# Attention probabilities normalised on ScalarE instead of GpSimd, with the attention's instruction lists reordered

## The chip, the cores and the metric

The kernel runs on one core of one Trainium2 chip. The metric is device time in microseconds (us) of one execution. Five engines of the core work here, each with its own list of instructions and bound to the others by semaphores: TensorE (PE: matmuls; PEld is its weight load), VectorE (DVE), ScalarE (ACT), GpSimd (POOL) and SyncE (SP), which issues nearly all DMAs.

## The reference, cut to what matters

A gated cross-attention layer and a gated feed-forward layer over x of 8 batches x 128 tokens x 512, in float32. There are 32 query heads of width 128 in 8 groups; each group shares one key and one value head.

```python
q = (layernorm(x) @ Wq)   # 8 x 32 heads x 128 tokens x 128
k = (ctx @ Wk); v = (ctx @ Wv)        # 8 heads each
q = q * cos + rotate_half(q) * sin    # rotary positions, k likewise
scores = einsum('bhqd,bhkd->bhqk', q, k) / sqrt(128)
scores = where(mask == 0, -1e9, scores)
attn = softmax(scores, axis=-1)
x = x + tanh(g_xattn) * (einsum('bhqk,bhkd->bhqd', attn, v).reshape(...) @ Wo)
x12 = layernorm(x) @ w12.T + b12      # then x1, x2 = split(x12)
x = x + tanh(g_ffn) * ((silu(x1) * x2) @ w3.T + b3)
```

## The kernel before, in words

Float32 products are made of three passes of a reduced format (fp32r): each operand is split into a high part `hi` (a copy on ScalarE into the format) and a low part `lo` (source minus hi, on GpSimd or VectorE), and `three` issues hi x hi, lo x hi and hi x lo. So every product costs three matmuls, and every operand one ScalarE copy and one subtraction.

A first stage (to about 118 us) makes the transposed inputs and all of k and v, and parks these in DRAM. Then comes the attention, written out by hand as one list of calls per engine; the position in that list is the only thing that sets the order of the work on an engine. Its piece is a unit: one batch and one group of four heads, 64 units in all, numbered n = 0 to 63; `u(n)` gives the arguments of unit n, and n = 16 gg + 2 c + k. The feed-forward layer follows from about 560 us.

For a unit the engines do, in the order of its data:

- TensorE: `q_block` (12 matmuls; 64 of them, block e needs the rotation of block e - 2 to be done), `scores` (3), `pv` (3), `out_proj` (12).
- VectorE: `cos_q` and `sin_q` (the rotation: one product, and two on 64 partitions), `score_blocks` (for units 4 to 51, whose scores come out transposed: 32x32 blocks are turned into `s_blk`), `mask_turned` (mask and row minimum into `prob`, four instructions) or, for the units outside of these, `mask_scores` (one add and four such instructions), `recip` (the reciprocal of the four row sums), `p_blocks` (32x32 blocks of `prob` turned into `p_blk`), `o_lo_split`, `add_out` (adds to the residual).
- ScalarE: `q_hi_copy`, `exps` (four exps of 128x128 in place in `prob`, with the row sums), `pT_hi_copy`, `o_hi_copy`, `split_chunk` (hi part of a weight chunk).
- GpSimd: `add_q` (sum of the cos and sin products), `q_lo_split`, `norm` (`prob` times the reciprocal of its row sum, one product of 128x512), `pT_lo_split`, and `split_chunk` (lo part of a weight chunk).
- SyncE: `store_s`/`load_s` and `store_p`/`load_p` send the turned blocks through DRAM and back, which finishes the transposition of scores and of probabilities; `next_k`, `next_v` and `load_next_chunk` fetch k, v and weights.

For units 0, 1 and 53 to 63 TensorE transposes `prob` itself (`prob_transpose`), and VectorE makes the lo part of pT. While an engine waits at one call of its list, all calls behind it wait. `prob`, `s_blk`, `p_blk`, q, pT and o have two slots each (k = 0 or 1), so unit n + 2 uses the slot of unit n. `recip` n waits for `exps` n, `norm` n for `recip` n, and `p_blocks` n or `prob_transpose` n for `norm` n.

The calls of the lists that the steps of the prediction touch, at the head of the attention:

```python
# TensorE: scores 0, q 4, q 5, scores 1, T 0, q 6, pv 0, scores 2, q 7, T 1, q 8, scores 3, q 9, pv 1,
#          scores 4, out 0, scores 5, q 10, q 11, pv 2, scores 6, out 1, scores 7, out 2, pv 3
# VectorE: cos_q(6), mask_scores 2, sin_q(6), cos_q(7), sin_q(7), pT_lo 1, recip 2, cos_q(8), sin_q(8),
#          o_lo 0, mask_scores 3, p_blocks 2, score_blocks 4
# GpSimd:  q_lo 2, chunk, add_q 5, norm 1, q_lo 3, chunk, add_q 6, chunk, add_q 7, norm 2, q_lo 4, add_q 8,
#          chunk, q_lo 5, add_q 9, norm 3, chunk, q_lo 6, pT_lo 2, chunk, norm 4, chunk, q_lo 7
```

In the feed-forward part `h_tile(b)` transposes a normalised batch on TensorE, `up(half, m)` is the first layer (24 matmuls), `silu`, `gate`, `gated_hi` and `gated_lo` make the operand of `down` (12 matmuls), and `result` adds the outcome to the residual; `up` i needs `gate` i - 2, and `down` n needs `result` n - 2.

Of the kernel before, what the change touches and what calls it, by code (L numbers as in the profile page):

```python
# [13 lines left out]
GH = H // KVH  # L14
# [64 lines left out]
def build(nc, x, ctx, pos, mask, g_x, g_f, Wq, Wk, Wv, Wo, w12, b12, w3, b3, out):  # L79
# [21 lines left out]
    with es:  # L101
# [105 lines left out]
        act_exp, dve_recip, pool_norm = sems("act_exp", "dve_recip", "pool_norm")  # L207
# [203 lines left out]
        def _(sp):  # L411
# [158 lines left out]
            def ffn_load(t):  # L570

                dst, s, _ = ffn_raw(t)
                if t < RAW:
                    sp.wait_ge(act_whi, CHUNKS - RAW + t + 1)
                    sp.wait_ge(pool_wlo, pool_split(CHUNKS - RAW + t))
                elif t == RAW:

                    sp.wait_ge(act_qhi, 4 * (UNITS - 1))
                    sp.wait_ge(pool_qlo, 4 * (UNITS - 1))
                for i in range(4):  # L580
                    sp.dma_start(dst[32 * i:32 * i + 32, :].rearrange("b (j f) -> b j f", j=4), ffn_src(t, i)).then_inc(s, 16)
            load_next_chunk(0)
            load_chunk(0, 2)
            next_k(0, 1)
            load_next_chunk(1)
            store_p(*u(2))
            store_s(4)
            load_next_chunk(2)
# [3 lines left out]
            store_s(5)  # L592
            load_s(5)
            load_next_chunk(3)
            load_next_chunk(4)
            load_p(*u(3))
            store_p(*u(4))
            store_s(6)
            load_p(*u(4))
            load_next_chunk(5)  # L600
            load_s(6)
            store_p(*u(5))
            store_s(7)
            load_p(*u(5))
            load_s(7)
            store_p(*u(6))
            store_s(8)
            load_p(*u(6))
            load_s(8)
            store_p(*u(7))  # L610
            store_s(9)
            load_p(*u(7))
            next_v(0, 1)
            load_s(9)
            load_next_chunk(6)
            store_p(*u(8))
            store_s(10)
            load_next_chunk(7)
            load_p(*u(8))
            next_k(1, 1)  # L620
            load_s(10)
            next_v(1, 1)
            store_p(*u(9))
            store_s(11)
            load_p(*u(9))
            load_s(11)
            store_p(*u(10))
            store_s(12)
            next_k(0, 2)
            load_s(12)  # L630
            load_p(*u(10))
            load_next_chunk(8)
            store_p(*u(11))
            store_s(13)
            load_next_chunk(9)
            load_p(*u(11))
            load_s(13)
            load_next_chunk(10)
            load_next_chunk(11)
# [4 lines left out]
            load_next_chunk(12)  # L644
# [4 lines left out]
            store_p(*u(14))  # L649
            load_next_chunk(13)  # L650
            store_s(16)
            next_v(0, 2)
            load_p(*u(14))
            load_s(16)
            store_p(*u(15))
            next_k(1, 2)
            store_s(17)
            load_p(*u(15))
            load_next_chunk(14)
            load_s(17)  # L660
            store_p(*u(16))
            load_next_chunk(15)
# [3 lines left out]
            next_v(1, 2)  # L666
            store_p(*u(17))
            store_s(19)
            load_p(*u(17))
            load_s(19)  # L670
            store_p(*u(18))
            store_s(20)
            load_next_chunk(16)
            load_next_chunk(17)
            load_s(20)
            load_p(*u(18))
            store_p(*u(19))
            next_k(0, 3)
            store_s(21)
            load_next_chunk(18)  # L680
            load_p(*u(19))
            load_s(21)
            store_p(*u(20))
            store_s(22)
            load_p(*u(20))
            load_next_chunk(19)
            load_s(22)
            store_p(*u(21))
            store_s(23)
            load_p(*u(21))  # L690
            load_s(23)
            load_next_chunk(20)
            next_v(0, 3)
            store_p(*u(22))
            store_s(24)
            load_next_chunk(21)
            load_p(*u(22))
            load_s(24)
            next_k(1, 3)
            store_p(*u(23))  # L700
            store_s(25)
            load_next_chunk(22)
            load_p(*u(23))
            load_s(25)
            load_next_chunk(23)
            store_p(*u(24))
            store_s(26)
            load_p(*u(24))
            load_s(26)
            store_p(*u(25))  # L710
            next_v(1, 3)
# [3 lines left out]
            store_p(*u(26))  # L715
            store_s(28)
            load_next_chunk(24)
# [5 lines left out]
            load_next_chunk(26)  # L723
            load_p(*u(27))
            load_s(29)
            store_p(*u(28))
            store_s(30)
            load_next_chunk(27)
            next_k(0, 4)
            load_p(*u(28))  # L730
            load_s(30)
            store_p(*u(29))
            store_s(31)
            load_next_chunk(28)
# [4 lines left out]
            store_s(32)  # L739
            load_next_chunk(29)  # L740
            load_p(*u(30))
# [3 lines left out]
            load_next_chunk(30)  # L745
            store_s(33)
            load_p(*u(31))
            load_s(33)
            store_p(*u(32))
            store_s(34)  # L750
            load_next_chunk(31)
            load_p(*u(32))
            load_s(34)
            store_p(*u(33))
            store_s(35)
            next_v(1, 4)
            load_p(*u(33))
            load_s(35)
            store_p(*u(34))
            store_s(36)  # L760
            load_next_chunk(32)
            load_p(*u(34))
            load_s(36)
            load_next_chunk(33)
            next_k(0, 5)
            store_p(*u(35))
            store_s(37)
            load_next_chunk(34)
            load_p(*u(35))
            load_s(37)  # L770
            store_p(*u(36))
            store_s(38)
            load_p(*u(36))
            load_s(38)
            load_next_chunk(35)
            load_next_chunk(36)
            store_p(*u(37))
            store_s(39)
            load_p(*u(37))
            load_s(39)  # L780
            next_v(0, 5)
            store_p(*u(38))
            store_s(40)
            load_p(*u(38))
            load_s(40)
# [2418 lines left out]
```

## Time and profile before

| what | value |
| --- | --- |
| median of 3 runs | 637.25 us (635.72 to 639.18) |
| the profiled execution: its own time | 636.77 us |
| the profiled execution: its span | 634.9 us |
| TensorE busy | 623.6 us, 98% |
| VectorE busy | 482.8 us, 76% |
| GpSimd busy | 450.3 us, 71% |
| ScalarE busy | 319.2 us, 50% |
| DMA | 118.38 MB, mean 186 GB/s |

A row of a group of instructions names the line, the engine, the operation, output<-inputs with their shapes and the count, then the busy time in us and the mean of one in ns, then the idle time of the engine just before them and what ended most of it. A row in order of time names the start in us, the duration in us, the engine, the line and the operation; in square brackets stands the idle time before it and its releaser. The line can be that of a helper: L889 to L891 are the three matmuls of `three`, L1422 is every hi copy, L1964 every lo subtraction on GpSimd, L2370 those on VectorE. Matmuls are pipelined and their ends are modelled, so the next one can start before the last one's end. "issue" as a releaser is time in which the engine waited for nothing that the profile shows; a wait for several semaphores can hide there.

### The profile page before, as it was taken

The page shows a single profiled execution, that of the slowest core. Times are in us where ns is not written, and L with a number is a line of the kernel's source. Part 1 is how long each engine was busy: PE and PEld are TensorE (multiplying, and loading weights), DVE is VectorE, ACT ScalarE, POOL GpSimd, SP SyncE. Part 2 cuts the span into 40 slices and gives each one's busy share as a digit, 9 for nine tenths or more (in the row PEclk, how much of TensorE's full clock was granted, in tenths as well). Part 3 has the DMA queues.
Part 4 walks back from the last instruction along what each step waited for, and adds up shares of the span by engine and source line. Part 5 has one row for each costly group of instructions (what it writes and reads, how often), then busy time and mean ns, then how long its engine had stood idle before and what let it go on. Part 6 is the DMA issues. An engine that isn't in the chain of part 4 may idle for free.

```text
span 634.9 us, 10094 instructions
## 1 busy us (share of the span) xinstructions
PE 623.6 (98%) x2865; PEld 511.7 (81%) x2865; DVE 482.8 (76%) x1235; ACT 319.2 (50%) x893; POOL 450.3 (71%) x374
## 2 busy tenths in 40 slices
PE   8999999998999999999999999999999999999997
PEld 7888888876888877787888788888778788888886
DVE  3987675797878878788878788878885998976342
ACT  5435622554764646455455555554634657545310
POOL 6456866898889898888898898988886677601100
PEclk9999999999999999999999999999999999999999
DMA  9997995156587686776677676876645413000002
GB/s 300 324 324 227 295 321 166 70 188 211 178 266 230 201 249 207 240 244 213 196 244 241 211 245 221 261 234 213 216 139 176 131 50 90 0 2 1 0 34 99
DMA packets 133990, 118.38 MB, mean 186 GB/s; under 512 B 9776, under 2 KB 104496, under 8 KB 133936
## 3 DMA queue, kind: packets, MB, share of 16 engines
q1 hardware_dynamic: 132512, 116.69, 57.7%
q0 software_dynamic: 384, 1.05, 0.5%
q8 instruction: 24, 0.39, 0.2%
q14 instruction: 30, 0.25, 0.1%
q10 hardware_dynamic: 1040, 0.00, 0.1%
HBM read 72.89 MB, written 44.83 MB: 185 GB/s over the span
## 4 chain that ended last, share of the span: by engine, by line
PE 69%; DVE 9%; POOL 8%; DMA 7%; issue 4%; ACT 3%; DVEq 0%; POOLq 0%; ACTq 0%; SPq 0%
PE f_bank L889 9%; PE f_bank L891 9%; PE f_bank L890 9%; PE o_bank L889 7%; PE o_bank L891 7%; PE o_bank L890 7%; DMA p<-p_scratch 3%; DVE t_sin L2417 3%; PE pv_bank L889 3%; PE pv_bank L891 3%; PE pv_bank L890 3%; PE s_banks L889 2%; PE s_banks L891 2%; PE s_banks L890 2%; ACT prob L1492 2%
## 5 line engine op out<-in xcount | busy, mean ns | idle before, releaser
L1492 ACT ACTIVATE prob<-prob,small 128x128 f32<-128x128 f32 x256 | 99.6, 391 | 42.0 <-DVE small L2516 27.9
L889 PE MATMUL f_bank<-xT_hi,wq_hi 128*128 128x512 f32 x256 | 100.4, 392 | 0.7 <-DVE t_sin L2417 0.6
L891 PE MATMUL f_bank<-xT_hi,wq_lo 128*128 128x512 f32 x256 | 99.8, 390 | 0.0
L890 PE MATMUL f_bank<-xT_lo,wq_hi 128*128 128x512 f32 x256 | 99.8, 390 | 0.0
L889 PE MATMUL o_bank<-wo_hi,o_hi 128*128 128x512 f32 x248 | 97.9, 395 | 0.5 <-issue 0.4
L891 PE MATMUL o_bank<-wo_hi,o_lo 128*128 128x512 f32 x248 | 97.0, 391 | 0.0
L890 PE MATMUL o_bank<-wo_lo,o_hi 128*128 128x512 f32 x248 | 96.7, 390 | 0.0
L2004 POOL TENSOR_TENSOR q<-t_cos,t_sin 128x512 f32<-128x512 f32 x64 | 83.2, 1304 | 14.1 <-DVE t_sin L2417 13.7
L2417 DVE TENSOR_TENSOR t_sin<-f_bank,rope 64x512 f32<-64x512 f32 x128 | 88.1, 688 | 2.3
L1964 POOL TENSOR_TENSOR q_lo<-q,q_hi 128x512 fp32r<-128x512 f32 x64 | 82.9, 1297 | 9.5 <-ACT q_hi L1422 9.3
L2019 POOL TENSOR_TENSOR pT_lo<-p,pT_hi 128x512 fp32r<-128x512 f32 x51 | 66.2, 1297 | 22.3 <-ACT pT_hi L1422 22.3
L2013 POOL TENSOR_TENSOR prob<-prob,small 128x512 f32<-128x512 f32 x64 | 66.7, 1042 | 20.7 <-DVE small L2547 19.9
L1422 ACT ACTIVATE pT_hi<-p 128x512 fp32r<-128x512 f32 x51 | 32.2, 631 | 68.5 <-DMA p<-p_scratch 68.3
L1422 ACT ACTIVATE o_hi<-pv_bank 128x512 fp32r<-128x512 f32 x64 | 37.8, 591 | 50.6 <-PE pv_bank L891 50.3
L889 PEld LDWEIGHTS o_bank<-wo_hi,o_hi 128*128 128x128 f32 x248 | 46.6, 188 | 13.0 <-issue 3.9
L889 PEld LDWEIGHTS f_bank<-xT_hi,wq_hi 128*128 128x128 f32 x256 | 48.1, 188 | 10.8 <-issue 0.8
L891 PEld LDWEIGHTS f_bank<-xT_hi,wq_lo 128*128 128x128 f32 x256 | 48.1, 188 | 10.1
L890 PEld LDWEIGHTS f_bank<-xT_lo,wq_hi 128*128 128x128 f32 x256 | 48.1, 188 | 9.8
L891 PEld LDWEIGHTS o_bank<-wo_hi,o_lo 128*128 128x128 f32 x248 | 46.6, 188 | 10.0
L2417 DVE TENSOR_TENSOR t_cos<-f_bank,rope 128x512 f32<-128x512 f32 x64 | 43.7, 684 | 14.0 <-PE f_bank L891 13.7
L890 PEld LDWEIGHTS o_bank<-wo_lo,o_hi 128*128 128x128 f32 x248 | 46.7, 188 | 9.4
L1422 ACT ACTIVATE q_hi<-q 128x512 fp32r<-128x512 f32 x64 | 39.3, 622 | 26.8 <-POOL q L2004 23.5
(185 smaller groups left out, 1439.4 us busy)
## 6 DMA issues: line engine op xcount, KB each, us to landing
p_scratch<-p_blk SPq DMA_DIRECT2D x51, 256.0 KB, 2.1
p<-p_scratch SPq DMA_DIRECT2D x51, 256.0 KB, 3.4
s_scratch<-s_blk SPq DMA_DIRECT2D x48, 256.0 KB, 2.2
s<-s_scratch SPq DMA_DIRECT2D x48, 256.0 KB, 3.4
k_scratch<-ks_parts SPq DMA_DIRECT2D x16, 512.0 KB, 3.1
raw<-in_L_xattn_Wq_dram SPq DMA_DIRECT2D x32, 256.0 KB, 3.9
raw<-in_L_xattn_Wo_dram SPq DMA_DIRECT2D x32, 256.0 KB, 3.5
k_parts<-k_scratch SPq DMA_DIRECT2D x16, 512.0 KB, 4.6
```

The lines of the kernel that those rows point to most:

```text
L889: nc.tensor.matmul(dst, st[0], mv_[0], start=start, stop=False)
L890: nc.tensor.matmul(dst, st[0], mv_[1], start=False, stop=False)
L891: return nc.tensor.matmul(dst, st[1], mv_[0], start=False, stop=stop)
L1422: nc.scalar.activation(dst, src, ACT.Copy).then_inc(s, 1)
L1492: e = nc.scalar.activation(prob[:, k, h, :], prob[:, k, h, :], ACT.Exp, bias=nmin[k][:, h:h + 1], scale=-1.0, accum_out=psum_row[k][:, h:h ...
L1964: nc.gpsimd.tensor_tensor(dst, a, b_, ALU.subtract).then_inc(s, 1)
L2004: nc.gpsimd.tensor_tensor(dst, c, s, ALU.add).then_inc(pool_rope, 1)
L2013: nc.gpsimd.tensor_tensor(prob[:, k], prob[:, k], rrow[k].unsqueeze(2).to_broadcast([128, GH, S]), ALU.mult).then_inc(pool_norm, 1)
L2019: nc.gpsimd.tensor_tensor(heads_by_q_block(pT_lo[:, k]), by_q_block(p32[:, k]), heads_by_q_block(f32(pT_hi[:, k])), ALU.subtract).then_inc ...
L2417: return nc.vector.tensor_tensor(dst, a, b_, ALU.mult)
```

## The change

`norm` moves from GpSimd to ScalarE. Where GpSimd made one product of 128x512 with the reciprocals broadcast, ScalarE makes four copies of 128x128, each with the reciprocal of its head as scale. The semaphore `pool_norm` becomes `act_norm`. All lists of the attention and of the feed-forward part are written anew for it, on all five engines: the same calls with the same arguments, moved by some places. On ScalarE norm n stands behind `exps` n, with none to four copies between.

```diff
@@ prob_transpose and p_blocks
-                pe.wait_ge(pool_norm, n + 1)
+                pe.wait_ge(act_norm, n + 1)
-                dve.wait_ge(pool_norm, n + 1)
+                dve.wait_ge(act_norm, n + 1)
@@ ScalarE
+            def norm(gg, c, k):
+                act.wait_ge(dve_recip, n_of(gg, c, k) + 1)
+                for h in range(GH):
+                    p = nc.scalar.activation(prob[:, k, h, :], prob[:, k, h, :], ACT.Copy, scale=rrow[k][:, h:h + 1])
+                p.then_inc(act_norm, 1)
@@ GpSimd
-            def norm(gg, c, k):
-                pool.wait_ge(dve_recip, n_of(gg, c, k) + 1)
-                nc.gpsimd.tensor_tensor(prob[:, k], prob[:, k], rrow[k].unsqueeze(2).to_broadcast([128, GH, S]), ALU.mult).then_inc(pool_norm, 1)
```

The lists of after, at the head of the attention (T is `prob_transpose`):

```python
# TensorE: scores 0, q 4, q 5, scores 1, T 0, q 6, scores 2, pv 0, q 7, T 1, q 8, scores 3, q 9,
#          scores 4, out 0, scores 5, pv 1, q 10, scores 6, q 11, pv 2, out 1, out 2, scores 7, pv 3
# VectorE: cos_q(6), sin_q(6), mask_scores 2, cos_q(7), sin_q(7), o_lo 0, pT_lo 1, cos_q(8), recip 2,
#          mask_scores 3, p_blocks 2, sin_q(8), score_blocks 4
# GpSimd:  q_lo 2, chunk, q_lo 3, chunk, add_q 5, add_q 6, chunk, add_q 7, q_lo 4, q_lo 5, chunk, chunk,
#          q_lo 6, chunk, add_q 8, pT_lo 2, add_q 9, q_lo 7
# ScalarE: norm 0, q_hi 2, q_hi 3, pT_hi 0, chunk, chunk, exps 1, o_hi 0, chunk, norm 1, pT_hi 1, exps 2,
#          q_hi 4, norm 2, chunk, chunk, q_hi 5, exps 3, norm 3, q_hi 6, mask fill, o_hi 1, chunk, q_hi 7,
#          pT_hi 2, exps 4, chunk, norm 4
```

A stretch of ScalarE's list in the middle, as a diff in order (before, then after):

```diff
-exps 25, chunk, pT_hi 24, o_hi 23, q_hi 28, q_hi 29, exps 26, pT_hi 25, chunk, chunk, o_hi 24, exps 27
+exps 25, chunk, norm 25, o_hi 23, q_hi 28, chunk, pT_hi 24, exps 26, q_hi 29, norm 26, pT_hi 25, chunk, o_hi 24, exps 27
```

In the feed-forward part TensorE's list has `up(0, 2)` ahead of `h_tile(4)` where it stood behind `h_tile(5)`, and VectorE's list has `result(0)` and `result(1)` behind `gated_lo(7)`. In the tail of the attention TensorE's list has `prob_transpose` 53, 54 and 55 ahead of the scores of two units on and of the q blocks that they stood behind.

## Rows read from the trace of the kernel before

**Rows 1.** The page's first part: busy us, share of the span, instructions.
```profile
PE 623.6 (98%) x2865; PEld 511.7 (81%) x2865; DVE 482.8 (76%) x1235; ACT 319.2 (50%) x893; POOL 450.3 (71%) x374
```

**Rows 2.** Busy us by stage: length; PE, PEld, DVE, ACT, POOL; clock; DMA, GB/s.
```profile
137.00:160.00 23.00, 20.74 (x89) 16.14 (x88) 18.40 (x50) 11.62 (x37) 19.08 (x17) 1.00 0.67 214
160.00:480.00 320.00, 317.37 (x1385) 257.45 (x1384) 264.20 (x745) 179.15 (x557) 277.69 (x229) 1.00 0.69 222
```

**Rows 3.** TensorE's table of waits: releaser, us in total, times, longest.
```profile
PE pv_bank L889 <- issue: 1.5, 3, 0.9
PE pv_bank L889 <- DVE o_lo L2370: 1.3, 3, 0.7
...
PE o_bank L889 <- issue: 0.4, 2, 0.2
...
PE s_banks L889 <- issue: 0.3, 1, 0.3
```

**Rows 4.** TensorE in order of time, in the head of the attention.
```profile
131.01 0.47 PE L889 MATMUL f_bank<-xT_hi,wq_hi 128*128 128x512 f32 x1 [0.63 <-DVE t_sin L2417]
...
138.70 0.47 PE L889 MATMUL s_banks<-q_hi,k_parts 128*128 128x512 f32 x1 [0.38 <-DVE small L2537]
...
149.40 0.47 PE L889 MATMUL pv_bank<-pT_hi,v_hi 128*128 128x512 f32 x1 [0.92 <-issue]
149.71 0.40 PE L890 MATMUL pv_bank<-pT_lo,v_hi 128*128 128x512 f32 x1
149.94 0.39 PE L891 MATMUL pv_bank<-pT_hi,v_lo 128*128 128x512 f32 x1
...
154.70 0.47 PE L889 MATMUL s_banks<-q_hi,k_parts 128*128 128x512 f32 x1 [0.97 <-POOL q_lo L1964]
```

**Rows 5.** GpSimd in order of time: pT_lo of unit 2.
```profile
148.01 1.29 POOL L2019 TENSOR_TENSOR pT_lo<-p,pT_hi 128x512 fp32r<-128x512 f32 x1
```

**Rows 6.** In order of time: unit 47's pT_lo on GpSimd, its pv on TensorE.
```profile
458.86 1.29 POOL L2019 TENSOR_TENSOR pT_lo<-p,pT_hi 128x512 fp32r<-128x512 f32 x1
...
460.25 0.47 PE L889 MATMUL pv_bank<-pT_hi,v_hi 128*128 128x512 f32 x1 [0.18 <-issue]
```

**Rows 7.** The page's groups of instructions: the exps, the sines, the norm.
```profile
L1492 ACT ACTIVATE prob<-prob,small 128x128 f32<-128x128 f32 x256 | 99.6, 391 | 42.0 <-DVE small L2516 27.9
...
L2417 DVE TENSOR_TENSOR t_sin<-f_bank,rope 64x512 f32<-64x512 f32 x128 | 88.1, 688 | 2.3
...
L2013 POOL TENSOR_TENSOR prob<-prob,small 128x512 f32<-128x512 f32 x64 | 66.7, 1042 | 20.7 <-DVE small L2547 19.9
```

**Rows 8.** ScalarE in order of time: a chunk's copy and the exps behind it.
```profile
265.09 0.62 ACT L1422 ACTIVATE wo_hi<-raw 128x512 fp32r<-128x512 f32 x1
265.61 0.40 ACT L1492 ACTIVATE prob<-prob,small 128x128 f32<-128x128 f32 x1
265.91 0.19 ACT L1492 ACTIVATION_READ_ACCUMULATOR prob<-prob,small 128x1 f32 x1
266.01 0.39 ACT L1492 ACTIVATE prob<-prob,small 128x128 f32<-128x128 f32 x1
```

**Rows 9.** ScalarE's table of waits.
```profile
ACT pT_hi L1422 <- DMA p<-p_scratch: 68.3, 34, 4.0
ACT o_hi L1422 <- PE pv_bank L891: 50.3, 31, 4.3
```

**Rows 10.** In order of time: ScalarE's pT_hi of unit 23, TensorE's pv behind it.
```profile
291.49 0.63 ACT L1422 ACTIVATE pT_hi<-p 128x512 fp32r<-128x512 f32 x1 [3.96 <-DMA p<-p_scratch]
...
294.52 0.47 PE L889 MATMUL pv_bank<-pT_hi,v_hi 128*128 128x512 f32 x1 [0.73 <-DVE o_lo L2370]
```

**Rows 11.** In order of time: gate(0) on VectorE, silu(1) on ScalarE.
```profile
572.38 0.74 DVE L2601 SCALAR_TENSOR_TENSOR t_sin<-f_bank,b_col,t_cos 128x512 f32<-128x512 f32 x1
...
575.50 0.69 ACT L1584 ACTIVATE t_cos<-s_banks,b_col 128x512 f32<-128x512 f32 x1 [0.78 <-PE s_banks L891]
```

**Rows 12.** ScalarE's groups: the one table load ahead of the attention.
```profile
L1422 ACT ACT_TABLE_LOAD x1 | 1.3, 1283 | 1.2 <-PEq L3192 1.2
```

More of the change, by code:

```diff
@@ L2795, in _ @@
             recip(*u(22))
+            add_out(*u(18))
             add_out(*u(19))
+            score_blocks(*u(24))
             p_blocks(*u(22))
-            score_blocks(*u(24))
             o_lo_split(*u(20))
@@ L2816, in _ @@
             o_lo_split(*u(22))
+            recip(*u(25))
             cos_q(0, 31)
-            recip(*u(25))
             sin_q(31)
             p_blocks(*u(25))
-            add_out(*u(22))
-            score_blocks(*u(27))
-            mask_turned(*u(26))
-            o_lo_split(*u(23))
-            recip(*u(26))
-            cos_q(0, 32)
-            sin_q(32)
+            mask_turned(*u(26))
+            score_blocks(*u(27))
+            o_lo_split(*u(23))
+            cos_q(0, 32)
+            recip(*u(26))
+            sin_q(32)
+            add_out(*u(22))
+            add_out(*u(23))
             p_blocks(*u(26))
-            add_out(*u(23))
             score_blocks(*u(28))
@@ L2833, in _ @@
             cos_q(0, 33)
+            sin_q(33)
             recip(*u(27))
-            sin_q(33)
+            add_out(*u(24))
             p_blocks(*u(27))
-            add_out(*u(24))
             score_blocks(*u(29))
@@ L2842, in _ @@
             recip(*u(28))
-            sin_q(34)
             p_blocks(*u(28))
+            mask_turned(*u(29))
+            score_blocks(*u(30))
             add_out(*u(25))
-            score_blocks(*u(30))
-            mask_turned(*u(29))
             o_lo_split(*u(26))
@@ L2965, in _ @@
             score_blocks(*u(45))
+            mask_turned(*u(44))
             o_lo_split(*u(41))
[L2967 removed]
             cos_q(0, 50)
[L2969 removed]
             recip(*u(44))
@@ L2972, in _ @@
             p_blocks(*u(44))
+            add_out(*u(40))
+            score_blocks(*u(46))
             add_out(*u(41))
-            score_blocks(*u(46))
             o_lo_split(*u(42))
@@ L3011, in _ @@
             o_lo_split(*u(47))
-            sin_q(55)
+            score_blocks(*u(51))
             p_blocks(*u(49))
-            score_blocks(*u(51))
             mask_turned(*u(50))
+            recip(*u(50))
+            add_out(*u(46))
             cos_q(0, 56)
-            recip(*u(50))
-            sin_q(56)
-            add_out(*u(46))
             p_blocks(*u(50))
             add_out(*u(47))
+            sin_q(56)
             mask_turned(*u(51))
```

1155 lines of the change are left out of this document (577 added, 578 removed).

## Prediction

> **What bounds the kernel now.** I read the busy shares of the engines first, then the same by stage, then TensorE's own waits, and last single stretches in order of time. TensorE is busy for 623.6 of 634.9 us [rows 1], at the full granted clock, and the head and the middle of the attention leave it only 2.3 and 2.6 us idle [rows 2]. So the change can't make the kernel faster by taking work off another engine; it can only remove moments in which TensorE stands still, or add some. Its table of waits and its rows in order of time hold them [rows 3, 4]. The reader adds up, in the attention and behind it: three waits of pv that the table puts down to issue, 1.5; three for the o_lo split, 1.3; one of 0.97, 0.63 and 0.38 each in the head; two of out_proj, 0.4; and three small ones of the scores of 0.3, 0.3 and 0.2, of which one row stands. That is 6.0 us in 14 waits. A wait costs more than its idle time. In a running stream a matmul starts 0.23 us after the one before, though it lasts 0.39; behind a wait the first lasts 0.47 and the second starts 0.31 later [rows 4]. Idle time is counted from the modelled end of the last matmul, 0.39 after its start, so each wait loses its idle time and 0.16 + 0.08 = 0.24 us more; 14 x 0.24 = 3.4. All that can be won is about 9.4 us, 1.5% of the time; the profiled execution took 636.77 us, and 627.4 would be its floor.
>
> **Where the waits lie.** Four are in the head, 0.63 + 0.38 + 0.92 + 0.97 = 2.90 us idle, with 0.24 each 3.9 us [rows 4]: q_block 8 at 131.01 waits for sin_q(6); scores 4 at 138.70 for mask_scores 3; pv 2 at 149.40, whose last input, pT_lo 2, starts at 148.01 and ends at 149.30 [rows 5]; scores 7 at 154.70 for q_lo 7. Two small ones follow at 460.25 and 461.49, of 0.18 and 0.31, 1.0 us in all; the first begins 0.1 us after GpSimd ended the pT_lo that it needs [rows 6], the second likewise after a q_lo. The three o_lo waits cost 2.0 in all. GpSimd is the fullest engine after TensorE: 277.69 of 320 us, 87%, in the middle, VectorE has 264.20, 83%, ScalarE 179.15, 56% [rows 2].
>
> **The norm itself.** Removed: 64 GpSimd products of 1042 ns, 66.7 us [rows 7], one for each unit. A unit has 12 + 3 + 3 + 12 = 30 matmuls 0.23 us apart, 6.9 us; GpSimd's load falls by 1.04 / 6.9, from 87% to 72%. Added: 256 ScalarE copies of 128x128, four a unit. The trace has no copy of that form with a scale read from a column. Bounds: four can't be quicker than one 128x512 copy, behind which the next instruction starts 0.52 us later; and they cost at most what four exps do, whose starts are 0.40 us apart with the readout of the sum between them, 1.6 us [rows 8]. The readout starts 0.30 us behind its exp, where a next copy would start; the exp has one column operand, as the new copy has. I take 4 x 0.30 = 1.2 us of ScalarE, nearest to that row, 77 us in all, and 1.3 us to the end of the last one.
>
> The Trainium skill speaks of that price too ("ScalarE: Activation LUTs", What ACT_TABLE_LOAD costs): an ACTIVATE has a fixed part of 186 ns, an operand read from a column adds 93 ns, an element 0.83 ns, and neighbours overlap by 93 ns. That is an estimate of 386 ns for one and 1.27 us for four, where the exp of the trace agrees with 391 ns [rows 7]; it speaks against four short instructions in the place of one. By it alone each unit's path grows by 0.2 us, and as that is covered (below) the sum stays what it is by the rows.
>
> What of it is on the path: unit n's path from scores to pv runs over s_blk, two DMAs, mask_turned, exps, recip, norm, p_blk, two DMAs, pT_hi, pT_lo. On GpSimd the norm had to wait for the operation in hand there, up to 1.3 us when it came at a bad moment. In the new ScalarE list it stands right behind its exps, mostly with nothing or one copy between. So + 0.2 us of work, and less queueing: the path gets no longer. What it adds is a wait inside ScalarE's list: norm n waits for recip n, which waits for exps n. Where VectorE is free that turn takes the 0.18 of the reciprocal and some 0.1 on each side, 0.4 us; where it is inside the two sines, up to 2 x 0.69 more [rows 7]. Queued behind it are q_hi, o_hi, pT_hi and the weight chunks; for these GpSimd and VectorE wait, and then TensorE. A unit now holds 0.56 x 6.9 = 3.9 us of ScalarE; + 1.2 + 0.4 makes 5.5, 80% of it. Now the engine idles 68.3 us for the loads of p and 50.3 for pv [rows 9], so there is room, but less of it.
>
> **The reordering in the head.** (1) sin_q(6) moves ahead of mask_scores 2, which is five VectorE operations: the wait of 0.63 is gone. (2) mask_scores 3 moves ahead of sin_q(8), so comes 1.4 us earlier, while scores 4 moves ahead of pv 1, 3 x 0.23 = 0.7 earlier: the wait of 0.38 is gone with 0.3 to spare. (3) pT_lo 2 loses norms 1, 2 and 3 ahead of it on GpSimd, 3.1 us, and p_blk 2 now precedes sin_q(8). But on ScalarE pT_hi 2 is moved behind norm 3, a mask fill, an o_hi, a chunk and a q_hi. Followed step by step with the durations above, pT_lo 2 ends at about 148 and pv 2 comes due about 147.3, with scores 6 now ahead of it: a wait of 0 to 0.6, with its restart up to 0.8. I take 0.8 and keep 0 for the range. (4) q_lo 7 loses norm 4 ahead of it, and scores 7 moves behind out_proj 2, 12 x 0.23 = 2.8 us: gone. The head gives -3.9 + 0.8 = -3.1.
>
> **The rest of the attention.** The two waits near 460: norms 47 and 48 no longer precede their pT_lo and q_lo, so up to -1.0; I take -0.8. Against that stands ScalarE. The model is the wait at 294.52: pT_hi had waited 3.96 us for its load, a chunk, a q_hi and o_hi were queued behind it, then o_lo, and pv lost 0.73 + 0.24 = 0.97 us [rows 10]. Each norm takes 1.6 us of the room in which such a backlog is caught up. I take one more such wait, rounded up to +1.1; the bounds are -2.0 (the three o_lo waits go) and +9.7 (ten of them, below). The other moves (out_proj, add_out, score_blocks, sines by a place, weight loads by up to two units, in the tail the transposes on TensorE ahead of scores) are covered: each operation keeps its unit, and a weight chunk is asked for some eight units, over 50 us, before it is read. A missed cover would show as a wait for raw, or as TensorE waiting for exps, and cost up to a norm, 1.3 us, once.
>
> **SyncE's queue.** Stores and loads of p and s keep their order, moved by a place at most; the k and v reloads and the chunks move past one or two of them. Each has about a unit, 6.9 us, in hand. Nothing; a late one would stop scores or pv once, for 1 to 3 us.
>
> **The feed-forward part.** up(0, 2) moves ahead of h_tile(4). It needs gate(0), which starts at 572.38, 3 us before up(0, 1) ends (silu(1), at 575.50, follows it) [rows 11]. h_lo(7) is then due with the end of up(0, 3), 24 x 0.23 = 5.5 us behind the last h_tile; three h_lo, gated_lo(0), a tile, gate(2) and a bias of about 0.7 each stand before it and leave some 0.7 us. result(0) goes behind gated_lo(7), some 4 us after the last up ends; down(2) needs it at 5.5. Nothing; without that cover up to 1 us each.
>
> **Sum.** -3.1 - 0.8 + 1.1 = -2.8 us: 636.77 - 2.8 = 633.97 for the profiled execution. The median of the runs, 637.25, lies 0.48 above it, so I predict 637.25 - 2.8 = 634.45, given as 634.4.
>
> **Rivals.** (B) No new waits, and the o_lo waits go as well, since a looser GpSimd lets TensorE's list run as planned: -3.1 - 0.8 - 2.0 = -5.9, 631.3. For it: GpSimd at 87%. Against it: such waits follow late loads, which no order cures. (C) The gain is handed back: four waits of the form of 294.52, 4 x 0.97 = 3.9, 637.2. For it: ScalarE at 80% in a fixed order. (D) Slower: ScalarE becomes the late engine. In its list pT_hi waits for a load 34 times, up to 4.0 us [rows 9], and the room behind such a wait shrinks by 1.6 us. From seven waits of 0.97 on, 6.8 against 3.9, the kernel is slower by 0.5%; ten give 9.7 - 3.9 = +5.8, 643.0. Against it: pT_hi n - 1 now stands mostly behind norm n, later in the unit, when its load has more often landed. (E) The change pays for switches between Exp and Copy, 128 table loads of 1.28 us, 164 us. Exps and copies alternate already and share one load [rows 12], so 1 in 100.
>
> **Chances.** The forecast 0.50 (own range 632.4 to 636.4), B 0.20, C 0.18, D 0.11, E 0.01. What a measurement of this kernel can tell from no change is about 0.5%, 3.2 us, so faster means below 634.06: all of B and 0.22 of the forecast's 0.50, 0.42. Slower are D, E and the upper end of C, 0.13. The rest is no difference, 0.45. The range goes from 630.8 to 638.8: it leaves out D and E (0.12) and the outer ends of B and C (0.06).
>
> **What would show it.** GpSimd's busy time falls by 66.7 us, ScalarE's rises by 77 to 100; the copies last about 0.39 us and start 0.30 apart. In TensorE's waits q_block 8, scores 4 and scores 7 are gone from the head and pv 2 is short or gone; waits for q_lo are gone; those for o_lo are as many or one more. If TensorE's waits sum to over 9 us of idle time, with o_lo and the loads of p in the chain behind them, D is right; if to under 1.5, B. The prediction is wrong from the ground up if the distance of the matmuls, 0.23 us, changes.

## The result, and the profile after

The changed kernel took 643.67 us (median of 7 runs, 639.34 to 645.14), the kernel before 637.98 beside it (7 runs): ratio 1.0091, interval 1.0067 to 1.0114. It is slower by 0.9%, 5.7 us, where 2.8 us less were forecast. Its profiled execution, 639.34 us with a span of 637.4, is the fastest of the seven; its trace shows 2.5 us of the loss, measured by the spans.

TensorE's granted clock tells a part of what the trace leaves out. Its mean over a run was 1.00 in three of the seven runs, the profiled one among them, and 0.996 or 0.997 in the other four, the median run among these; all 69 runs of the kernel before in the later rounds had 0.999 or 1.00. A run at 0.997 holds a short stretch at the lower of the clock's two levels, 1.2 instead of 2.4 GHz, which cost some 1.6 us in the one trace taken apart below (e5).

The page's line of busy times of the kernel after, and the group of the moved norm (the columns as ahead of the prediction):

```profile
PE 623.1 (98%) x2865; PEld 511.5 (80%) x2865; DVE 484.9 (76%) x1235; ACT 394.1 (62%) x1149; POOL 386.4 (61%) x310
...
L1499 ACT ACTIVATE prob<-prob,small 128x128 f32<-128x128 f32 x256 | 81.7, 391 | 13.9 <-DVE small L2549 13.8
```

ScalarE gained 74.9 us of work and GpSimd lost 63.9 [rows 1]; a copy lasts 391 ns, and the four of one unit stand in time as

```profile
344.75 1.28 ACT L1499 ACTIVATE prob<-prob,small 128x128 f32<-128x128 f32 x4 [0.25 <-DVE small L2549]
```

so the work moved at the forecast price (1.2 us a unit and 1.3 to its end), and the wait for the reciprocal is 13.8 us in 30 waits for all 64 units, half of the 0.4 us a unit that I had allowed. The loss lies elsewhere. The same two stages as [rows 2], of after:

```profile
137.00:160.00 23.00, 22.78 (x99) 17.89 (x98) 19.26 (x52) 16.85 (x52) 18.81 (x15) 1.00 0.75 239
160.00:480.00 320.00, 312.17 (x1360) 252.45 (x1359) 258.74 (x724) 229.37 (x731) 225.90 (x179) 1.00 0.70 221
```

In the head TensorE idles 0.2 us where it idled 2.3: the forecast gain is there. In the middle it idles 7.8 us where it idled 2.6. TensorE's table of waits of after (releaser, us in total, times, longest), against [rows 3]:

```profile
PE o_bank L889 <- issue: 3.2, 6, 1.4
PE pv_bank L889 <- DVE o_lo L2372: 2.6, 2, 2.3
PE o_bank L889 <- ACT o_hi L1422: 1.7, 1, 1.7
...
PE pv_bank L889 <- issue: 0.5, 2, 0.2
```

The waits are few and some are long, before out_proj and pv. The chain of waits of after, ahead of the two longest (start, us, what); first to out_proj at 235.91, which waited 1.7 us, then to pv at 350.44, which waited 2.3:

```profile
223.93 6.52 DMA p_scratch<-p_blk
...
230.46 2.97 DMA p<-p_scratch
...
233.99 0.61 ACT q_hi L1422
234.60 0.49 ACT o_hi L1422
...
235.91 0.47 PE o_bank L889
```
```profile
339.42 4.94 DMA s_scratch<-s_blk
...
344.38 3.17 DMA s<-s_scratch
...
348.50 0.62 DVE p_blk L2560
349.12 0.60 DVE s_blk L2503
349.72 0.59 DVE o_lo L2372
...
350.44 0.47 PE pv_bank L889
```

Both begin at a store of p or s that landed late, 6.52 and 4.94 us after its issue, against a median of 2.1 and 2.2 in the kernel before. An engine's fixed list does the rest: ScalarE stood at pT_hi for the reload of p, with q_hi and the o_hi of another unit queued behind it; VectorE stood at the mask for the reload of s, with p_blk, s_blk and o_lo behind it. SyncE's own list in order of time says what was on the way when the first of these stores was issued:

```profile
221.74 0.57 SPq L498 DMA_DIRECT2D raw<-in_L_xattn_Wo_dram  x1
222.96 0.37 SPq L543 DMA_DIRECT2D s<-s_scratch  x1
223.38 0.50 SPq L456 DMA_DIRECT2D k_parts<-k_scratch  x1
223.93 0.43 SPq L512 DMA_DIRECT2D p_scratch<-p_blk  x1
```

A weight chunk (256 KB), a reload of s (256 KB) and the keys (512 KB) were issued within 2.2 us ahead of the store. The page's DMA rows say that stores land later in general. Kernel before, then after (count, KB each, median us from issue to landing):

```profile
p_scratch<-p_blk SPq DMA_DIRECT2D x51, 256.0 KB, 2.1
p<-p_scratch SPq DMA_DIRECT2D x51, 256.0 KB, 3.4
s_scratch<-s_blk SPq DMA_DIRECT2D x48, 256.0 KB, 2.2
s<-s_scratch SPq DMA_DIRECT2D x48, 256.0 KB, 3.4
```
```profile
p_scratch<-p_blk SPq DMA_DIRECT2D x51, 256.0 KB, 2.6
p<-p_scratch SPq DMA_DIRECT2D x51, 256.0 KB, 3.1
s_scratch<-s_blk SPq DMA_DIRECT2D x48, 256.0 KB, 2.8
s<-s_scratch SPq DMA_DIRECT2D x48, 256.0 KB, 3.2
```

In the lists themselves, between the stores of units 8 and 46, 57 or 58 loads of weights, keys and values have these neighbours in SyncE's list:

| kernel | behind a unit's reloads, ahead of the next stores | between the two stores | behind the stores, ahead of the reloads | between the two reloads |
|---|---|---|---|---|
| before | 20 | 8 | 22 | 7 |
| after | 34 | 7 | 8 | 9 |

So the first theory is: the new list puts the bulk loads ahead of the stores, the stores land late, and now and then TensorE waits. The rivals: ScalarE is too full (D of the prediction); or the new lists of the engines don't fit each other whatever the transfers do.

### The profile page after: what moved, and what is told of

It reads as the page before. It is cut to its first block, busy times and chain, and to the rows that moved or that the text cites. A ratio compares the mean times of both kernels' runs of the same rounds, so it can differ in the third digit from the quotient of the medians.

```text
span 637.4 us, 10287 instructions
## 1 busy us (share of the span) xinstructions
PE 623.1 (98%) x2865; PEld 511.5 (80%) x2865; DVE 484.9 (76%) x1235; ACT 394.1 (62%) x1149; POOL 386.4 (61%) x310
## 4 chain that ended last, share of the span: by engine, by line
PE 83%; DVE 7%; DMA 6%; issue 2%; ACT 1%; POOL 1%; SPq 0%; DVEq 0%; ACTq 0%
PE f_bank L889 11%; PE f_bank L891 11%; PE f_bank L890 11%; PE o_bank L889 9%; PE o_bank L891 8%; PE o_bank L890 8%; PE pv_bank L889 3%; PE pv_bank L891 3%; PE pv_bank L890 3%; PE s_banks L889 3%; PE s_banks L891 3%; PE s_banks L890 3%; DMA s_scratch<-s_blk 2%; DVE t_sin L2419 1%; PE t_bank L889 1%
## 5 line engine op out<-in xcount | busy, mean ns | idle before, releaser
L1492 ACT ACTIVATE prob<-prob,small 128x128 f32<-128x128 f32 x256 | 99.6, 391 | 47.9 <-DVE small L2518 40.0
L1499 ACT ACTIVATE prob<-prob,small 128x128 f32<-128x128 f32 x256 | 81.7, 391 | 13.9 <-DVE small L2549 13.8
L2372 DVE TENSOR_TENSOR o_lo<-pv_bank,o_hi 128x512 fp32r<-128x512 f32 x64 | 43.5, 680 | 7.0 <-ACT o_hi L1422 6.6
```

What stands on the lines that cost most here:

```text
L1492: e = nc.scalar.activation(prob[:, k, h, :], prob[:, k, h, :], ACT.Exp, bias=nmin[k][:, h:h + 1], scale=-1.0, accum_out=psum_row[k][:, h:h ...
L1499: p = nc.scalar.activation(prob[:, k, h, :], prob[:, k, h, :], ACT.Copy, scale=rrow[k][:, h:h + 1])
L2372: nc.vector.tensor_tensor(dst, src, f32(hi_part), ALU.subtract).then_inc(s, 1)
```

## The experiments

Each ratio is to the kernel before, run beside it on the same chip.

**The lists, one at a time.** e1 and e2 exchange SyncE's whole list between the kernels, the feed-forward loads and the order of stores and reloads included; e3 takes the move back out of the new lists and gives GpSimd its old one, and e4 makes the move alone in the old ones.

```diff
# e1: after, its SyncE list replaced by that of before; e2: before, with that of after
# e3: after, but norm is GpSimd's product again, and GpSimd's list that of before
# e4: before; GpSimd's list without its norms, and on ScalarE:
             exps(*u(n))
+            norm(*u(n))      # one call later for units 2 and 52
```

> The changed kernel, with SyncE's list of before put back; all else as changed. Theory ScalarE (its list is too full, o_hi comes late behind any late load): nothing is mended, 643 to 645. Theory SyncE (in the new list weight, k and v loads are issued in bunches ahead of the stores and loads of p and s, whose round trips then take up to 6.5 us): the late round trips go, and the head's gain of 3 us stays, 633 to 636. Theory TensorE and VectorE lists (less distance between a unit's steps): 643 to 645.

> The kernel before, with only SyncE's list of the changed kernel. Theory SyncE: the late round trips appear here too, 641 to 645. Theory ScalarE, and theory TensorE and VectorE lists: as before, 637 to 639.

> The changed kernel's lists on SyncE, TensorE, VectorE and ScalarE, but the norm is the one GpSimd product again: its calls are taken out of ScalarE's list, and GpSimd has its list of before. Theory ScalarE: the room is back, 634 to 638. Theory SyncE: stays at 641 to 645. Theory TensorE and VectorE lists: stays at 641 to 645.

> The kernel before with all its lists, but norm n on ScalarE as four scaled copies straight behind exps n (one call later for units 2 and 52), and taken out of GpSimd's list. Theory ScalarE: slower than before by 4 to 7 us, 642 to 645, with o_hi and o_lo in the waits. Theory SyncE, and theory TensorE and VectorE lists: not slower, 634 to 638, as GpSimd's waits near 150 and 460 go and SyncE's order is the old one.

| kernel | median us | ratio, interval |
|---|---|---|
| e1_after_old_sync | 653.30 | 1.0275, 1.0239 to 1.0311 |
| e2_before_new_sync | 666.99 | 1.0498, 1.0462 to 1.0535 |
| e3_after_norm_gpsimd | 706.38 | 1.1106, 1.1077 to 1.1135 |
| e4_before_norm_scalar | 657.63 | 1.0330, 1.0301 to 1.0358 |

None of the four came out in a range that any theory had given for it. These exchanges cost 17 to 70 us, many times what is to be explained. They say that the lists belong together; they don't say which one lost the 5.7 us. e4 says one thing more: in the old lists the move costs 21 us, in the new ones 5.7, so the reordering took back most of its price. Where e4 lost it: TensorE's waits of that kernel, and its stages 160 to 480 and 480 to 560 (idle 7.2 and 8.0 us; before 2.6 and 0.5), and ScalarE's wait for the reciprocals, 39.4 us where after has 13.8.

```profile
PE pv_bank L889 <- DVE o_lo L2372: 8.8, 8, 1.8
```
```profile
160.00:480.00 320.00, 312.81 (x1360) 253.25 (x1359) 258.84 (x723) 229.87 (x723) 229.17 (x181) 1.00 0.69 220
480.00:560.00 80.00, 71.97 (x367) 58.62 (x367) 60.02 (x182) 55.72 (x182) 41.06 (x34) 1.00 0.33 95
```
```profile
ACT prob L1499 <- DVE small L2549: 39.4, 63, 4.8
```

**ScalarE's work and its wait, by themselves.** e5 leaves out most of the normalisation (one copy of 128x4 a unit, the wait kept; the probabilities stay unnormalised). e8 adds four copies of 128x128 a unit to the kernel before, from tiles that nobody changes, with no wait. e9 adds the wait and no work.

```diff
# e5, in after                                     # e8, in before, behind exps 4 to 51
-  for h in range(GH): ... prob[:, k, h, :]        +  for h in range(GH):
+  for h in range(1):  ... prob[:, k, h, 0:4]      +      nc.scalar.activation(junk[:, k, h, :], mfill[:, h, :], ACT.Copy, scale=tg_x)
# e9, in before, where e4 has its norms
+  act.wait_ge(dve_recip, n_of(gg, c, k) + 1)
```

> The changed kernel with the norm cut to one copy of 128x4 (only four probabilities of the first head are scaled, the rest stays unnormalised); wait for recip and all lists kept. ScalarE has 0.9 to 1.0 us less of work for each unit. Theory ScalarE work: 633 to 637, the o_hi and o_lo waits mostly gone. Theory DMA (late landings of the p and s stores behind bunched loads): 640 to 643, since the landings don't change.

> The kernel before, norm on GpSimd, with four copies of 128x128 more on ScalarE straight behind the exps of units 4 to 51 (mfill scaled into an unused region; nobody waits for them, they wait for nothing). It is the work of the moved norm without its wait: 48 x 1.2 = 58 us of ScalarE. Theory ScalarE work: slower by 4 us or more, up to the +21 of the norm moved in the old lists. Theory that the wait for recip is what hurts: within 2 us of before.

> The kernel before with its lists and with the normalisation on GpSimd; ScalarE only waits, behind each block of exps, until VectorE has the reciprocals of the row sums (at the places where e4_before_norm_scalar had its four copies). Theory, the wait costs: moving the copies in the old lists cost 21 us although the same amount of ScalarE's work with no wait cost 2.5 us (e8), so this kernel is slower by 10 to 20 us (647 to 657), and the trace shows some 30 to 40 us of waits for the reciprocals on ScalarE. Rival, it is the copies' coming late on ScalarE, or GpSimd's list without them, that cost the 21 us: then this kernel is within 3 us of before (under 640).

| kernel | median us | ratio, interval |
|---|---|---|
| e5_after_short_norm | 640.73 | 1.0078, 1.0048 to 1.0108 |
| e8_before_extra_copies | 639.06 | 1.0036, 1.0011 to 1.0061 |
| e9_before_wait_only | 641.59 | 1.0072, 1.0046 to 1.0098 |

With next to no work of the norm left, the changed kernel is still slower than before by 0.8%; the intervals of e5 and of after overlap. In the kernel before, the same work, for 48 of the 64 units, costs 2.3 us and the wait 4.6 (these two intervals overlap as well). So D, a ScalarE too full, falls as the whole account: the work explains no more than a part of the loss. e8 came out between my two ranges, just above the one for work that hurts nobody (within 2 us). For e9 I had said two things. The time was a miss, 4.6 us and not 10 to 20; the waits were not. The trace books 33.5 us under the reciprocal (L2614), spread over what stands behind it, o_hi 12.2, pT_hi 9.4, the weight chunks' and q's copies the rest. So the 30 to 40 us of waits are there, and most of them cost TensorE nothing. Work and wait by themselves make 7 of e4's 21 us; what makes the rest, of which 7.5 us more idle time stand in the stage 480 to 560, stays open. The clock has a share: e4's six runs have means of 0.992 to 0.999.

e5's trace shows what a long wait costs beyond its idle time, a rival to all accounts by waits alone. TensorE stood for 2.03 us ahead of an out_proj; then the clock fell (the first matmul behind the wait, then a row of busy times by stage as above, with the clock third from its end):

```profile
291.50 0.61 PE L889 MATMUL o_bank<-wo_hi,o_hi 128*128 128x512 f32 x1 [2.03 <-issue]
...
292.00:295.00 3.00, 3.00 (x9) 2.32 (x8) 2.43 (x5) 1.19 (x6) 0.23 (x1) 0.50 0.45 135
```

The matmuls of that stretch start 0.43 us apart, not 0.23. From 291.50 to 295.22 nine of them took 3.72 us, where 2.15 would do at the full clock (0.31 behind the wait, then 8 x 0.23): 1.6 us more for one wait. All four runs of e5 have a mean of 0.997, so part of what it has left is the clock's, and it is no clean price of the norm's work. Not each such wait is followed by it: behind the 2.27 us at 350.44 the trace of after stays at 1.00.

**The traffic.** e6 and e7 load only a quarter of each weight chunk of the attention (the rest of the chunk keeps old values), in after and in before; every issue, wait and place stays.

```diff
-                sp.dma_start(dst, wq_src(G, o) if o < 4 else wo_src(G, o - 4)).then_inc(raw_loaded[o], 16)
+                src = wq_src(G, o) if o < 4 else wo_src(G, o - 4)
+                if o < 4: dst, src = dst[:, 0:1], src[:, 0:1]
+                else:     dst, src = dst[:, 0:128], src[:, 0:128]
+                sp.dma_start(dst, src).then_inc(raw_loaded[o], 16)
```

> The changed kernel with each weight chunk of the attention loaded only to a quarter (the rest of the slot keeps stale weights, so the projections are of other weights); same number of DMAs, same order. Theory DMA: the landings of the p and s stores fall back to 2 to 3 us, longest under 4, and the time to 631 to 635. Theory ScalarE work: 640 to 644.

> The control: the kernel before with the weight chunks loaded to a quarter (stale weights, as in the other). Both theories: 1 to 3 us faster than before, 634 to 637, since its longest waits behind late loads go. If it gains as much as the changed kernel does by the same edit, the loads are no reason for the difference between the two.

| kernel | median us | ratio, interval |
|---|---|---|
| e6_after_small_weights | 632.83 | 0.9945, 0.9926 to 0.9964 |
| e7_before_small_weights | 634.74 | 0.9964, 0.9943 to 0.9986 |

These two part the theories. Less traffic gives the changed kernel 1.5% (1.0091 to 0.9945, 9.3 us) and the kernel before 0.4% (2.3 us), with every instruction of the engines at its place. In e6 the medians to landing are 2.1 and 2.1 us for the stores, 2.9 and 3.0 for the reloads, and the middle idles 2.7 us, as before:

```profile
160.00:480.00 320.00, 317.30 (x1390) 258.61 (x1389) 263.35 (x738) 233.26 (x745) 230.35 (x182) 1.00 0.62 198
```

So the loss hangs on transfers, and with these lighter the new lists are no worse than the old, by the medians 1.9 us better (the two intervals overlap).

**The places of the loads.** The order of the stores and reloads stays in each of these; only where the loads of weights, keys and values stand between them changes. e11 and e12 exchange the places, which changes the order among some loads too; e10, e13, e17 and e18 arrange them anew in after, e14 in before, between units 8 and 48.

```diff
# e10, one load behind the two stores, a second behind both reloads
-            load_next_chunk(16)
             store_p(*u(19))
             store_s(21)
+            load_next_chunk(16)
             load_s(21)
-            load_next_chunk(17)
             load_p(*u(19))
-            next_k(0, 3)
+            load_next_chunk(17)
             store_p(*u(20))
             store_s(22)
-            load_next_chunk(18)
+            next_k(0, 3)
             load_p(*u(20))
# e11: after, each load behind the same store or reload as in before; e12: before, as in after
# e13: as e10, the second between the two reloads;  e14: the rule of e10 in before
# e17: as e10, the second beside the first, behind the stores
# e18: after, only the loads right ahead of a store moved, behind the stores
```

> The changed kernel with one edit in SyncE's list, between units 8 and 48: loads of weight chunks, of keys and of values that stood ahead of a p or s store, or two and three together, stand one at a time behind the two stores of a unit; the order of the stores and reloads themselves stays. Theory, bunched loads delay the stores: the sum of the store round trips between 140 and 475 us falls from 314 towards 265 us, TensorE's waits in the middle fall by 3 to 5 us, and the time is 637 to 640. If it is below before, it is the better kernel. Rival, the loads are as many and wherever they stand they cost the same, or come too late for the split: 643 to 648.

> The changed kernel; its own order of p and s stores and reloads, but each load of weights, keys and values stands behind the same store or reload as in the kernel before. It parts e1_after_old_sync (the whole old list of SyncE, +2.75%) in two. Theory, where the loads stand sets the round trips, and the old places suit stores: the sum of round trips falls to 270 to 290 us and the time is 638 to 644. Rival, the loads' order must suit the splits of the new lists: as slow as e1, 648 to 655.

> The kernel before with its own order of p and s stores and reloads, but each load of weights, keys and values behind the same store or reload as in the changed kernel. Theory, bunched loads delay the stores: the sum of the round trips rises from 265 to 285 to 310 us, and the time by 3 to 8 us (640 to 645). Rival, the order of stores and reloads is what mattered: within 2 us of before (635 to 639), and e2_before_new_sync's 30 us are that order's.

> As e10_after_loads_behind, but where two loads are due in a unit the second stands between its two reloads, not at its end ahead of the next unit's stores. Theory, what is left of the late landings in e10 (seven stores with a load within 2.5 us ahead of them) goes: the sum of round trips falls from 273 to 255 to 268 us and the time to 633 to 636. Rival, the reload behind the second load now lands later, or later loads hold up the splits: 637 to 642.

> The kernel before with the same rule in SyncE's list as e10_after_loads_behind. Theory, the old list has few bunched loads (265 us of round trips against 273 in e10), so the rule has nothing to give there: 634 to 639, and e10's 6.8 us are the repair of the new list. Rival, the rule is a gain of its own in any list: 629 to 633, and the move of the normalisation with its lists would then still be a loss of 4 us or more beside it.

> As e10_after_loads_behind, but where two loads are due in a unit both stand together behind its two stores, ahead of both reloads; none stands between the reloads or behind them. Theory, stores want nothing ahead of them, and SyncE waits there for the first store's landing anyway: 633 to 637. Rival, what e13 showed (a reload issued right behind a load landed 6.1 us later) holds for both reloads behind such a pair: 639 to 646.

> The changed kernel with only those loads moved behind the stores that stood right ahead of a store; those between two reloads stay there. Theory, the loads ahead of stores are the cause and e10's other moves do nothing: 635 to 638, as e10. Rival, the loads must also leave the place between the reloads, as e13 (643.65) has many there and e10 none: 640 to 645.

The places are counted as in the table above (ahead of the stores / between them / behind them / between the reloads). "Round trip" is the median of a store to landing plus that of its reload, for p and for s, from the DMA rows of the stretch 160 to 480.

| kernel | places | round trip p, s, us | median us | ratio, interval |
|---|---|---|---|---|
| before | 20 / 8 / 22 / 7 | 5.4, 5.6 | 636 to 638 | 1 |
| after | 34 / 7 / 8 / 9 | 6.0, 6.0 | 643.67 | 1.0091, 1.0067 to 1.0114 |
| e10_after_loads_behind | 21 / 0 / 36 / 0 | 5.4, 5.7 | 636.85 | 1.0006, 0.9991 to 1.0022 |
| e17_after_loads_in_pairs | 0 / 0 / 57 / 0 | 6.0, 5.9 | 640.73 | 1.0064, 1.0043 to 1.0084 |
| e18_after_only_ahead_moved | 0 / 0 / 48 / 9 | 6.1, 6.2 | 642.99 | 1.0089, 1.0058 to 1.0120 |
| e13_after_loads_spread | 0 / 0 / 37 / 19 | 5.9, 5.7 | 643.65 | 1.0126, 1.0100 to 1.0153 |
| e11_after_old_places | 21 / 9 / 21 / 7 | 5.6, 6.1 | 646.44 | 1.0144, 1.0119 to 1.0169 |
| e14_before_loads_behind | 20 / 0 / 37 / 0 | 5.4, 5.6 | 640.76 | 1.0060, 1.0037 to 1.0083 |
| e12_before_new_places | 28 / 8 / 7 / 15 | 5.1, 5.7 | 650.37 | 1.0223, 1.0193 to 1.0253 |

e10 is the edit that answers the question. Nothing but the places of loads in SyncE's list differs from after, and the loss is gone: 1.0091 to 1.0006. (I had expected 637 to 640 us of it; it took 636.85.) The medians to landing are those of before again; the DMA rows of its page, its middle stage, and what is left of TensorE's waits:

```profile
p_scratch<-p_blk SPq DMA_DIRECT2D x51, 256.0 KB, 2.1
p<-p_scratch SPq DMA_DIRECT2D x51, 256.0 KB, 3.4
s_scratch<-s_blk SPq DMA_DIRECT2D x48, 256.0 KB, 2.2
s<-s_scratch SPq DMA_DIRECT2D x48, 256.0 KB, 3.5
```
```profile
160.00:480.00 320.00, 314.50 (x1376) 255.77 (x1375) 261.35 (x730) 231.36 (x736) 227.44 (x180) 1.00 0.70 222
```
```profile
PE o_bank L889 <- issue: 2.5, 3, 1.7
PE pv_bank L889 <- DVE o_lo L2372: 1.8, 2, 1.5
```

SyncE's own waits say the same: for the p stores to land 57.2 us in after, 24.0 in e10. But they give no more than the time of before. The middle idles 5.5 us, 2.3 less than in after and 2.9 more than before, which is about what the head has won. The spans of the two traces differ by 3.3 us (637.4 and 634.1), the ratios by 5.4. The clock has a part in that: one of e10's twelve runs has a mean as low as 0.997, and four of after's seven.

One thing e10 did not mend: the two longest waits stand where they stood in after, before the same out_proj and pv, 1.73 us at 235.93 (1.69 in after) and 1.46 at 347.79 (2.27). Ahead of both the store now lands in 2.0 and 2.3 us, and it is the reload of s that lands late, 5.77 and 4.98 us after its issue. The chain of the first:

```profile
222.80 5.77 DMA s<-s_scratch
...
235.93 0.47 PE o_bank L889
```

With small weights (e6) 1.2 us of that first wait are still there, and each of the traces of e5, e13, e17 and e18 has one of 0.9 to 2.2 us there. So the new lists have a spot at which a late landing reaches TensorE, be it a store's or a reload's.

e14 is its control: the same rule in the old list costs 4.1 us, more than I had expected (634 to 639 us). So e10 repairs the new list and is no gain of its own.

e18, e13 and e17 correct the theory, and its sentence "stores want nothing ahead of them". e18 took every load from ahead of the stores and won nothing; its stores land quickly again (2.2 us), but its reloads take 3.8 and 3.9 where after has 3.1 and 3.2. What was taken from the store was given to the reload. e13 has 19 loads between the reloads, and one chain of its trace shows the price; a weight load issued at 222.97 and the reload of s right behind it:

```profile
222.97 0.50 SPq L498
...
223.57 6.14 DMA s<-s_scratch
...
234.20 0.53 ACT pT_hi L1422
...
235.25 0.49 ACT o_hi L1422
...
237.07 0.47 PE o_bank L889
```

Of the arrangements of after that I tried, e10 has the shortest round trips and the best time: at most one load behind the stores and one at the unit's end. That it is the even spacing that helps is a reading and not shown. e10 has about as many loads ahead of the stores as before (21 and 20), and over the kernels made from after the ratio rises with neither place alone. Against a rule by places speaks e11, which has the counts of before in the new order of stores and reloads; it took 646.44 us, outside both ranges that I had given, and is slower than after. Of the seven edits of places only e17 and e18 landed in a range given beforehand, that of the rival to my theory.

The round trip is not the whole account. e12 has the round trips of before and loses 2.2%; e14 has them and loses 0.6%; e13 loses twice what e17 does, with no longer ones. For e13 and e17 the clock has a share: four of e13's six runs have a mean of 0.995 to 0.997, of e17's six one. For e12 the trace names the single landing. Its three longest waits, 2.0, 2.1 and 2.3 us, all stand before an out_proj and carry no releaser in TensorE's table, but `out_proj` needs o_lo, and VectorE's rows say what that waited for. SyncE, VectorE and TensorE ahead of the longest:

```profile
395.63 0.43 SPq L461 DMA_DIRECT2D v_lo<-v_scratch  x1
396.16 0.38 SPq L543 DMA_DIRECT2D s<-s_scratch  x1
...
400.49 0.29 DVE L2516 CUSTOM_DVE_ANT_1 prob<-s_banks,s 128x128 f32<-128x128 f32 x1 [1.60 <-DMA s<-s_scratch]
...
401.34 0.69 DVE L2370 TENSOR_TENSOR o_lo<-pv_bank,o_hi 128x512 fp32r<-128x512 f32 x1
...
402.12 0.47 PE o_bank L889
```

A reload of s was issued right behind the two value loads and landed some 4.3 us later; the mask stood for it, o_lo behind the mask, and out_proj for o_lo. The wait of 2.1 us at 307.68 has the same form (value loads at 299.98 and 300.52, the reload of s at 301.06, the mask at 306.04 behind 2.44 us of waiting), and the one at 226.87 too, with a reload of p in the place of the value loads. The wait of 1.4 us at 421.93 in after is of this kind as well. So a median over all round trips can't show the loss: it depends on the few transfers behind which an o_lo or o_hi is queued. How much of 2.2% these make in the other runs of e12 was not followed up.

## Why the prediction was wrong

**Held.** TensorE's matmuls are 0.23 us apart still, and it is the bound, 98% busy. The work: 74.9 us more on ScalarE, 63.9 less on GpSimd, 0.39 us a copy, 0.30 apart. The Trainium skill's page "ScalarE: Activation LUTs" (What ACT_TABLE_LOAD costs) gave by estimate 386 ns and 1.27 us for four, and the trace agrees, 391 ns and 1.28 us. Table loads (E) did not come. The head: forecast -3.1 us; TensorE's busy time between 137 and 160 rose by 2.0 and up to 137 by 0.2, with pv 2 waiting 0.2 where I had 0.8 with its restart. The feed-forward part: "Nothing", and no wait of over 0.3 us is in it. The condition that I had set for D, over 9 us of waits in all with o_lo and loads of p in the chain, was all but met, 7.8 in the middle. Of the two waits near 460 that were to go, only the second went; pv still waits 0.25 us at 460.20, against 0.18.

**Failed: "SyncE's queue. ... Nothing".** I looked at whether a moved load would come too late for its own reader, where it has a unit in hand, and not at what a moved load does to the transfers behind it. The stores and reloads of p and s are the path of each unit. In the new list 34 instead of 20 loads stand ahead of a unit's stores; the stores land 0.5 to 0.6 us later at the median, and up to 6.8 us after their issue (5.3 in before). Placing the same loads anew, with nothing else changed (e10), took 0.85% off, 5.4 of the 5.7 us. The price that I had put at nothing is that. It is a price of the places together and not of the place ahead of the stores: e18 cleared that one and won nothing.

**Mis-sized: "one more ScalarE-backlog wait, +1.1".** The mechanism of [rows 10] was right, a late reload in front of a fixed list, then o_hi, o_lo and pv or out_proj. The middle lost 5.2 us of idle time, the longest waits by it, where I had 1.1 less the 0.8 at 460. I had also priced a wait at its idle time and 0.24 us; behind a long one the clock can add 1.6 (e5). I took the number of late reloads from the old list and put the change on ScalarE's room; what changed was which landings were late and what was queued behind them. The first bound, +9.7 for ten such waits, holds the true value, but I priced it by ScalarE's work, which cost 2.3 us in the old lists (e8) and by e5 about 0.8 in the new (1.0091 to 1.0078, inside the noise). D came near in time (643.0) for a reason that was not its own.

**B fell, but not for my reason.** "Such waits follow late loads, which no order cures" stood against B. They follow late landings, and the order of issue changes these: e10 took 2.3 us of idle time out of the middle.

**Not foreseen: the price of a gain in the head.** Even e10, with landings as before, idles 2.9 us more in the middle, and is level with before; its forecast gain of 2.8 us is not there. ScalarE's own wait and work, 4.6 and 2.3 us in the old lists, may be what takes it, and so may the late reloads that e10 still has; the repaired list was not run without the one or the other, so this stays open.

## What to carry to other kernels

Where one queue carries both short round trips on the path and bulk loads with slack, a bulk load's place is part of the round trip's price: before moving one, look not only at who reads it but at which store or reload is issued behind it, and compare the medians to landing, kernel by kernel. Then follow each long wait of the bounding engine back to its one late transfer, as the medians alone misled here. Moving the bulk load from ahead of the store to ahead of the reload moved the cost and didn't remove it (e18). The best places found here, one load behind the stores and one at the unit's end, cost 0.6% in the other kernel's list (e14), so they are no rule. Lists written out for five engines are one object: to test one part of such a change, keep all lists and alter sizes (smaller loads, shorter work) rather than exchange one list. And look at the mean clock of every run before pricing a wait by its idle time alone.

## What the runs showed of the hardware that I had not expected

A scaled copy of 128x128 with its scale in a column takes what an exp of that shape takes, 391 ns; the four of a unit end 1.28 us after their start, 0.24 us more than the one GpSimd product that they replace (1042 ns, [rows 7]). Stores of 256 KB on one queue, with DMA 70% busy over the stage, landed in 2.1 us at the median, and in 6.5 where 1 MB had been issued within 2.2 us ahead. A wait alone, with no work behind it and the engine half idle, cost the kernel 4.6 us (e9), by the medians twice as much as 1.2 us of work in each of 48 units (e8). And behind a stand of 2.03 us TensorE's granted clock was 0.50 for over 3 us (e5), in e12 0.57 from 308 to 312 us behind one of 2.11, while it stayed at 1.00 behind one of 2.30 in the same trace.
